# Four recurrent layers: the first head's keys are copied during the projections, the maxima's rows once, and layer 0's V product moves between the first fills

## The reference

```
xn = layernorm(x)
# layer 0
q, k, v = xn @ Wq + bq, xn @ Wk + bk, xn @ Wv + bv      # 16 heads of 8
attn = softmax(q @ k.T / sqrt(8));  s = (attn @ v) @ Wo + bo
g = silu(tanh(xn @ weight @ aux1 @ aux2 + bias))
x = x + s * g
# layers 1 and 2: other attentions and feed-forwards, not touched by the change
# layer 3
q, k, v = rope(xn @ qw), rope(xn @ kw), xn @ vw          # 16 heads of 8
s = (causal_softmax(q @ k.T / sqrt(8)) @ v) @ ow;  g = silu(top1_experts(xn))
x = x + s * g
```

## Time and profile before

| | us |
|---|---|
| median of 3 runs | 2002.25 |
| the three runs | 1996.25, 2002.25, 2002.73 |
| profiled execution, its own time | 1996.94 |
| its span, first to last instruction | 1995.1 |
| PE busy in the span | 1650.5 (83%) |
| DVE busy | 1448.0 (73%) |
| ACT busy | 1112.2 (56%) |

### The profile page before, as it was taken

How to read it: one execution, slowest core, us unless ns; L and a number is a source line. 1 busy time by engine, 2 the same in 40 slices (tenths; PEclk the granted TensorE clock), 3 DMA queues, 4 the chain that set the end, 5 groups by cost and what they waited for, 6 DMA issues and landing times. The chain is left out here.

```text
span 1995.1 us, 29288 instructions
## 1 busy us (share of the span) xinstructions
PE 1650.5 (83%) x10105; PEld 666.2 (33%) x10105; DVE 1448.0 (73%) x2724; ACT 1112.2 (56%) x2262; POOL 313.7 (16%) x464
## 2 busy tenths in 40 slices
PE   3689999999999976799987986881659888999877
PEld 2212222222222214344444444771412222222246
DVE  5689999999999905855556056336768889999825
ACT  3258888888888881322212533342306666777744
POOL 0102100100010000000003345313012222111123
PEclk9779999999999997999987988886759999999989
DMA  4001111211110021063223587531501111111132
GB/s 132 32 20 63 66 51 45 73 61 46 46 61 32 4 47 66 5 127 94 93 105 112 154 285 252 184 114 49 182 33 46 47 41 45 42 45 52 32 78 69
DMA packets 80283, 156.07 MB, mean 78 GB/s; under 512 B 20476, under 2 KB 37756, under 8 KB 76440
## 3 DMA queue, kind: packets, MB, share of 16 engines
q1 hardware_dynamic: 65394, 123.90, 19.3%
q0 software_dynamic: 14384, 29.29, 4.9%
q10 hardware_dynamic: 358, 1.01, 0.2%
HBM read 104.33 MB, written 48.89 MB: 77 GB/s over the span
## 5 line engine op out<-in xcount | busy, mean ns | idle before, releaser
L855 ACT ACTIVATE heads_probs<-heads_pS 128x512 f32<-128x512 f32 (+3 forms) x1664 | 822.5, 578 | 217.9 <-PE heads_pS L768 195.5
L880 DVE TENSOR_REDUCE heads_run_max<-heads_pM 128x1 f32<-128x1024 f32 x512 | 601.0, 1219 | 37.0 <-PE heads_pM L742 29.1
L786 PE MATMUL heads_pO<-heads_probs,heads_vh 128*32 128x512 f32 (+2 forms) x3328 | 446.3, 583 | 2.1 <-ACT heads_probs L855 1.4
L768 PE MATMUL heads_pS<-heads_qs,heads_ks 59*128 59x512 bf16 (+3 forms) x1040 | 310.5, 371 | 30.4 <-ACT heads_probs L855 16.0
L742 PE MATMUL heads_pM<-heads_ks,heads_qs 56*128 56x512 bf16 (+3 forms) x1040 | 281.8, 380 | 17.3 <-DVE heads_run_max L891 7.1
L891 DVE TENSOR_REDUCE heads_run_max<-heads_pM 128x1 f32<-128x512 f32 x384 | 246.6, 684 | 18.9 <-PE heads_pM L742 17.8
L742 PE MATMUL heads_pM<-heads_ks,heads_q_first 56*128 56x512 bf16 x624 | 173.3, 397 | 44.1 <-DMA heads_ks<-k_parts_dram 25.8
L768 PE MATMUL heads_pS<-heads_q_first,heads_ks 59*128 59x512 bf16 x624 | 183.6, 376 | 23.8 <-ACT heads_probs L855 18.9
L768 PEld LDWEIGHTS heads_pS<-heads_qs,heads_ks 59*128 59x128 bf16 x1040 | 77.8, 94 | 321.6 <-ACT heads_probs L855 278.6
L888 DVE CUSTOM_DVE_ANT_0 heads_masked_out<-heads_pM,heads_mask_end 128x128 bf16<-128x128 f32 (+3 forms) x256 | 121.0, 486 | 28.5 <-PE heads_pM L742 26.1
L1616 DVE TENSOR_REDUCE second_row_max<-second_banks 128x1 f32<-128x2048 f32 (+15 forms) x16 | 20.7, 1291 | 156.0 <-PE second_banks L1574 77.5
(11 more groups left out here) (384 smaller groups left out, 2139.5 us busy)
## 6 DMA issues: line engine op xcount, KB each, us to landing
top_weights<-k_comb_dram SPq DMA_DIRECT2D x128, 128.0 KB, 3.0
second_w<-in_L_W_dram SPq DMA_DIRECT2D x12, 1024.0 KB, 10.0
heads_ks<-k_parts_dram SPq DMA_DIRECT2D x124, 96.0 KB
k_hid_slots_dram<-k_zeros SPq DMA_DIRECT2D x8, 1152.0 KB, 4.5
k_h_slots_dram<-second_work SPq DMA_DIRECT2D x48, 192.0 KB
second_work<-k_hid_slots_dram SPq DMA_DIRECT2D x48, 192.0 KB
heads_qs<-k_parts_dram SPq DMA_DIRECT2D x40, 192.0 KB
k_parts_dram<-proj_part SPq DMA_DIRECT2D x12, 512.0 KB, 4.7
```

Of the source, the lines that this page charges most:

```text
L768: mm = pe.matmul(pS[:, slot, 0:c1 - c0], ks[c % ROUND][rows, u * P:(u + 1) * P], qs[c % ROUND][rows, c0:c1], start=True, stop=not diag)
L786: mm = pe.matmul(pO[k * 32:k * 32 + VW, int(second), o:BLK], vh[c][:, t, :], probs[u % 2][:, k * BLK + o:(k + 1) * BLK], start=first_chunk ...
L855: act.activation(probs[u % 2][:, k * BLK + c0 - b * BLK:(k + 1) * BLK], pS[:, slot, 0:c1 - c0], ACT.Exp)\
L880: dve.reduce_max(run_max[:, i, blocks[0][0] // 2:blocks[0][0] // 2 + 1], both.rearrange("p k c -> p (k c)"), AX.X).then_inc(taken, 2)
```

## The change

- The first head's keys go into a buffer `K.first_k` during the projections. As each part of k is split, SP copies its eight rows from the part's own tile, once for each place in the stack and for either half: 6 + 6 + 2 DMAs of 8 rows, each group ahead of that part's store. Their ones are set by POOL in the projections. `load_first_keys` and DVE's ones are gone from the head stage.
- Fills always read rows 64 and up, scores rows 0 and up; `turns` is gone. So the maxima's rows are written to the lower half only (three DMAs per head instead of six), and ones are set there only. Both halves of q and k are still loaded.
- Layer 0's V product leaves the projections and becomes four more steps of `FirstFeedForward` (16 steps instead of 12), each of sixteen 128-column matmuls with the bias through the identity, copied by ACT. Three steps stand ahead of the first fill instead of six. POOL takes V only when all steps are done.
- The masks' swapped copies are made for the lower half only.

```diff
@@ -123,9 +122,8 @@
             dve.tensor_scalar(K.neg_above[:, :], masks[:, 0, :], NEG, None, ALU.mult).then_inc(made, 1)
             dve.tensor_scalar(K.neg_below[:, :], masks[:, 1, :], NEG, None, ALU.mult).then_inc(made, 1)
 
-            for to, at in ((slice(0, HALF), slice(HALF, P)), (slice(HALF, P), slice(0, HALF))):
-                dve.tensor_copy(K.ident_swapped[to, :], K.ident[at, :]).then_inc(made, 1)
-                dve.tensor_scalar(K.neg_below_swapped[to, :], masks[at, 1, :], NEG, None, ALU.mult).then_inc(made, 1)
+            dve.tensor_copy(K.ident_low[:, :], K.ident[HALF:P, :]).then_inc(made, 1)
+            dve.tensor_scalar(K.neg_below_low[:, :], masks[HALF:P, 1, :], NEG, None, ALU.mult).then_inc(made, 1)
 
 
 class Norm:
...
+                        for dst, src in first_keys(K, parts[1][a], a):
+                            sp.dma_start(dst, src).then_inc(K.first_loaded[bool(rope)], 16)
                     sp.dma_start(K.parts[w][:, a, :, :], parts[w][a][:, :]).then_inc(stored[w], 16)
                     if rope and (w, a) == (1, 0):
                         load_first_queries(sp)
             for w in range(2):
                 sp.wait_ge(stored[w], 16 * PARTS)
+
+        @block.gpsimd
+        def _(pool):
+            pool.memset(K.first_k[HALF // 2:HALF, :], 1.0).then_inc(ones_in, 1)
 
         @block.tensor
         def _(pe):
...
@@ -374,7 +382,7 @@
                 project(n)
             if rope:
                 pe.wait_ge(routing.counted, 1)
-            for t in range(NT):
+            for t in range(NT if rope else 0):
                 if t % TPB == 0 and t >= 2 * TPB:
                     pe.wait_ge(vkept, t // TPB - 1)
                 mm = pe.matmul(pv[:, t // TPB % 2, t % TPB * P:(t % TPB + 1) * P], K.xnT[:, t * P:(t + 1) * P],
@@ -462,11 +470,6 @@
                     for i, at in enumerate(ROUTE_AT):
                         if at == n:
                             routing.dve_step(dve, i)
-            if not rope:
-                for c in range(NB):
-                    dve.wait_ge(vproj, c + 1)
-                    dst, src = v_block(c)
-                    dve.tensor_tensor(dst, src, bv.unsqueeze(1).broadcast_to([P, TPB, D]), ALU.add).then_inc(vkept, 1)
 
 
 def query_loads(K, h):
...
@@ -487,6 +490,14 @@
     for half in (0, HALF):
         for row, end, src in query_loads(K, 0):
             yield K.first_q[half + row:half + end, :], src
+
+
+def first_keys(K, kept, part):
+
+    n, at = PRODUCTS[part], sum(PRODUCTS[:part]) * HD
+    for half in (0, HALF):
+        for k in range(n):
+            yield K.first_k[half + at + k * HD:half + at + (k + 1) * HD, :], kept[0:HD, :]
 
 
 def causal_plan(causal):
...
         last_stored = S.sem("last_stored")
...
         SECOND = sorted({(k, b) for _, k, _, b, _, _, second in chunks if second})
...
@@ -596,17 +607,11 @@
                 for row, end, src in key_loads(K, h):
                     yield ks[c % ROUND][half + row:half + end, :], src, stacked[c % ROUND]
 
-        def load_first_keys(queue, turn):
-            half = (0, HALF)[turn]
-            queue.wait_ge(ones_set[0], turn + 1)
-            for row, end, src in key_loads(K, 0):
-                queue.dma_start(ks[0][half + row:half + end, :], src).then_inc(stacked[0], 16)
-
         def split_max(queue, g):
 
             queue.wait_ge(splitting, 4 * g + 1)
             if g > 0:
-                queue.wait_ge(rows_in, 32 * PARTS * g)
+                queue.wait_ge(rows_in, 16 * PARTS * g)
             queue.tensor_copy(max_parts[:, 0, :], neg_max[:, :]).then_inc(splitting, 1)
             queue.wait_ge(splitting, 4 * g + 2)
             queue.tensor_tensor(left[:, :], neg_max[:, :], max_parts[:, 0, :], ALU.subtract).then_inc(splitting, 1)
...
@@ -638,10 +643,9 @@
         @block.sync
         def _(sp):
             def load_max_rows(c):
-                for row in (STK, HALF + STK):
-                    for a in range(PARTS):
-                        sp.dma_start(qs[c % ROUND][row + a:row + a + 1, :].rearrange("o (t c) -> o t c", c=P),
-                                     max_rows[a * NT:(a + 1) * NT, :]).then_inc(rows_in, 16)
+                for a in range(PARTS):
+                    sp.dma_start(qs[c % ROUND][STK + a:STK + a + 1, :].rearrange("o (t c) -> o t c", c=P),
+                                 max_rows[a * NT:(a + 1) * NT, :]).then_inc(rows_in, 16)
 
             def one_head(p, c):
                 if exists(p, c + 2):
...
@@ -657,13 +661,12 @@
                     sp.dma_start(dst, src).then_inc(sem, 16)
 
 
-            load_first_keys(sp, 0)
-            sp.wait_ge(ones_set[1], 2)
+            sp.wait_ge(ones_set[1], 1)
             for dst, src, sem in load_stacks(0, 1):
                 sp.dma_start(dst, src).then_inc(sem, 16)
             sp.wait_ge(exped, 1)
             load_max_rows(0)
-            sp.wait_ge(ones_set[2], 2)
+            sp.wait_ge(ones_set[2], 1)
             every_head(one_head)
             for c in range(ROUND):
                 sp.wait_ge(ot_stored[c], 16 * STORES * len(range(c, LAST, ROUND)))
...
@@ -707,15 +710,16 @@
                     scatter.finish(pool)
 
             for i in range(1, ROUND):
-                for n, row in enumerate((HALF // 2, HALF + HALF // 2)):
-                    pool.memset(ks[i][row:row + HALF // 2, :], 1.0).then_inc(ones_set[i], 1)
-                    pool.wait_ge(ones_set[i], n + 1)
+                pool.memset(ks[i][HALF // 2:HALF, :], 1.0).then_inc(ones_set[i], 1)
+                pool.wait_ge(ones_set[i], 1)
             for i in range(ROUND):
                 pool.memset(vh[i][:, :, HD:VW], 0.0).then_inc(zeroed, 1)
             pool.wait_ge(zeroed, ROUND)
             for i in range(ROUND):
                 pool.memset(vh[i][:, :, HD:HD + 1], 1.0).then_inc(v_preset, 1)
             pool.wait_ge(v_preset, ROUND)
+            if feed:
+                pool.wait_ge(feed.ffn_kept, feed.STEPS)
             take_v(0, 0)
             if not causal:
                 split_max(pool, 0)
...
@@ -733,12 +735,12 @@
                 n = BLOCKS * (ROUND * p + c) + before[j + 1]
                 i, blocks, _ = runs[j]
                 if j == 0:
-                    pe.wait_ge(stacked[c % ROUND], 16 * LOADS * (p + c // ROUND + 1))
+                    loads = LOADS * (p + c // ROUND + 1) + (FIRST_LOADS - LOADS if c % ROUND == 0 else 0)
+                    pe.wait_ge(stacked[c % ROUND], 16 * loads)
                 if not isinstance(n, int) or n > FILLED:
                     pe.wait_ge(taken, n - FILLED)
                 for k, (b, w) in enumerate(blocks):
-                    at = next(turns)
-                    rows = slice(at, at + STK)
+                    rows = slice(HALF, HALF + STK)
                     mm = pe.matmul(pM[:, bank_of(c, j, k), 0:w], qs[c % ROUND][rows, i * P:(i + 1) * P],
                                    ks[c % ROUND][rows, b * BLK:b * BLK + w], start=True, stop=True)
                 mm.then_inc(filled, 1)
...
@@ -759,17 +761,16 @@
                 e = EVENTS * h + place(p, c, n) + 1
                 slot = (EVENTS * c + place(p, c, n) + 1) % RING
                 if n == 0:
-                    pe.wait_ge(rows_in, 32 * PARTS * (h + 1))
+                    pe.wait_ge(rows_in, 16 * PARTS * (h + 1))
                 if not isinstance(e, int) or e >= RING:
                     pe.wait_ge(exped, e - RING + 1)
                 diag = causal and c0 == u * P
-                at = next(turns)
-                rows, mask = slice(at, at + STK + PARTS), slice(at, at + HALF)
+                rows, mask = slice(0, STK + PARTS), slice(0, HALF)
                 mm = pe.matmul(pS[:, slot, 0:c1 - c0], ks[c % ROUND][rows, u * P:(u + 1) * P],
                                qs[c % ROUND][rows, c0:c1], start=True, stop=not diag)
                 if diag:
                     pe.matmul(pS[:, slot, 0:P], K.ident_b[mask, :], K.neg_below[mask, :], start=False, stop=False)
-                    mm = pe.matmul(pS[:, slot, 0:P], K.ident_swapped[mask, :], K.neg_below_swapped[mask, :], start=False,
+                    mm = pe.matmul(pS[:, slot, 0:P], K.ident_low[:, :], K.neg_below_low[:, :], start=False,
                                    stop=True)
                 mm.then_inc(scored, 1)
 
...
@@ -809,7 +810,7 @@
                                 turn(p, c + 1, (EVENTS * (ROUND * p + c) + TURN_AT + 1, (EVENTS * c + TURN_AT + 1) % RING))
                             score_chunk(p, d, n)
 
-            AT_ONCE = 6
+            AT_ONCE = 3
             for m in range(AT_ONCE if feed else 0):
                 feed.pe_step(pe, m)
             pe.wait_ge(preset, 1)
...
@@ -957,11 +955,13 @@
             w, moving = ((K.w["L0_ffn_weight"], K.xnT), (K.w["L0_ffn_aux_weight1"], self.probs[0]))[n]
             mm = pe.matmul(self.ring[:, m % ring, :], w[:, :], moving[:, cols], start=True, stop=True)
         else:
+            still, w, bias = ((self.probs[1], K.w["L0_ffn_aux_weight2"], K.row["L0_ffn_bias"]),
```

(14 more changed lines are left out.)

29 lines of the change are left out of this document (14 added, 15 removed).

## The result

The changed kernel takes **1973.15 us** (median of 4 runs, 1972.4 to 1979.2) beside 2002.49 for the kernel before (4 runs, 1996.25 to 2003.7): ratio **0.9869, interval 0.9847 to 0.9891**, faster by 1.3%. The forecast was 1974. Its profiled execution took 1973.72 (span 1971.9), 23.2 us less than before's.

A forecast was written before the change was run, and what follows sets the result against it. It took a 2.39 us ring through ACT and PE as the bound, plus late maxima rows and slow starts. Terms -16.0 - 0.9 - 7.3 = -24.2 from 1996.94 gave 1972.7; 1.3 on top made 1974 us, range 1964 to 1989.

The forecast's parts named there:

- The rows (-16.0): Heads of layers 0 and 3: three maxima DMAs instead of six remove PE's waits, 9.0 plus 7.0 us.
- The margin of 1.9 us: At each head's change: three row issues take 2.9 us where six needed 4.8, leaving 1.9 us spare.
- Fixed halves at no cost in the unit: Heads' units of fills and scores: fixed halves cost 0, with 0.12 us margin, and the unit stays 2.39 us.
- The rival of pairs on one half: Heads of layers 0 and 3: same-half pairs delay the fourth score, 37 us in all, 2011 us; chance 0.06.
- Layer 0's projections (+3.7): Layer 0's projections: fourteen key copies on SP and crowded DMA engines delay the head stage to 56.0, +3.7 us.
- the first rival: Projections of layers 0 and 3: copies at 1.2 us per issue start both stages 10 us later, 1985 to 1990; chance 0.13.
- Layer 0's start (-9.35 + 4.8): Layer 0's head stage: first fill 9.35 us sooner after stage start, then 4.8 us lost to feed steps and halves.
- the warm slots: Layer 0's first fills: warmer early slots return about 1 us of the loss.
- Layer 3's start (-7.3): Layer 3's start: stage start 4.7 us later, first fill 12.0 sooner within the stage, net -7.3 us.
- the -12.0: Layer 3's head stage: DVE ready at 1453.7, where before the first fill ran at 1465.72, -12.0 us.
- The bound of -4: Layer 3's start: the weaker bound on its net gain, -4 us, if issues take 0.75 us.
- Sum: Whole kernel: rows, layer 0's start and layer 3's start add to -24.2 us, giving 1972.7 for the profiled execution.

The follow-up runs named there:

- e9: The kernel before, unchanged, run again with a trace in the third group: ratio 1.0006 to the kernel before.
- e10: The changed kernel, unchanged, run again with a trace in the third group: ratio 0.9869 to the kernel before.
- e1: The kernel before with fixed halves and three rows of maxima instead of six, nothing else: ratio 0.9957 to the kernel before.
- e2: The changed kernel with the maxima's rows written to both halves again, six DMAs per head: ratio 0.9903 to the kernel before.
- e3: The changed kernel with layer 0's V product back in the projections, twelve feed-forward steps: ratio 0.9880 to the kernel before.
- e4: The changed kernel with fills on the lower half too, where the scores are: ratio 1.569 to the kernel before.
- e5: The changed kernel with the stores of k's three parts ahead of all fourteen key copies on SP: ratio 0.9880 to the kernel before.
- e7: The changed kernel with the first head's queries also copied from part tiles, copies shared among SP, ACT and POOL: ratio 0.9882 to the kernel before.
- e6: The changed kernel with fills on both halves in turn until the first score: ratio 0.9848 to the kernel before.
- e12: The kernel before with fixed halves alone, still six rows of maxima: ratio 1.0054 to the kernel before.

## Why the prediction was right, and where not

**The rows (-16.0): measured -16.3 on the heads from the first transpose on (-8.2 and -8.1).** The size is right for this pair of executions; in e9 and e10 layer 0's fourteen periods give 8.9, as here 8.7, but layer 3's heads 14.3, since the kernel before takes 407.3 us there and not 401.2. Three rows are enough for it: e1's fourteen periods take 541.55 although packets of code still fall 0.7 to 6.9 us behind the first twelve of its transposes and its third row lands up to 3.4 us after its issue. The margin of 1.9 us took them up, as reckoned. The cause was given wrongly. I wrote of "anything that slows one issue", and read the issue of 3.43 us at 1544.78 as SP's own. In fact a load of program code kept one engine of the sixteen; the row whose packets queue behind it lands late, in layer 3 SP's next issue waits as well, and which head is hit depends on where the code's loads fall. And it was not asked what else of the change moves them: with V between the fills nearly all have moved away, so that even six rows don't stall in layer 0 (e2). Either of the two, three rows (e1) or the rest of the change (e2), removes layer 0's 9 us; together they give them once. That the whole gain came out near 16 although its cause was misread is in part luck. In the whole change three rows are therefore needed only for some 3 to 5 us of layer 3 (397.6 in e2 against 393 to 395). That the place of the packets and not the level of that group did it is supported by e1 and e3, of the same group, whose packets fall on the rows as in the kernel before.

**Fixed halves at no cost in the unit: right.** 38.62 per undisturbed head in every trace but e4's. The rival of pairs on one half fell; its price appears where I had not put it, in e4, where the granted clock stays at 0.50 with it.

**Layer 0's projections (+3.7): measured +4.5**, stage start 52.31 to 56.83. The sum was near for wrong terms, which is luck. Issues cost 0.79 us each and not 0.5 (most 0.62 to 0.67, two of them 1.3 and 1.5), so the last store left at 50.59 and not near 46.6. It landed in 5.3 and not in 10.7 us: the first queries' last packets (queue q10) move between 53 and 54 us as in the kernel before, so the later store meets only the end of them, while e5's last store, issued at 38.95, took 10.9 again. That is half of the first rival's mechanism without its size. (That rival's own sum does not come out: 10 us later in both stages is 20 and not 12 to 15, so 1994, outside the range.) The Trainium skill, "DMA: Bandwidth & Descriptors", section "Issuing engines are not separate DMA queues", calls the issue time "usually small relative to the DMA itself". For one DMA the trace agrees, 0.58 us of issue against 5.3 of landing for the last store; but fourteen issues on one queue add up to 11.12 us, and that set the end. By the same section of the Trainium skill, issuing from several engines saves only the issue time. In e7 it gained 5 us in layer 3, and in layer 0 the issues themselves grew longer and it lost 5.

**Layer 0's start (-9.35 + 4.8): measured -10.05 and +4.1.** The first fill comes 4.80 us after the stage starts, and from there to the first transpose it is 44.88 us instead of 40.80. The terms: V was 1.4 and is 2.2 by e3; halves were 3.2 + 1.2 = 4.4 and are 3.6 by e6; 5.8 less 4.1 leaves 1.7 for the warm slots, which no run shows alone. The warm clock was a small term of -1 in my sum. e12 shows that it counts for more: without the early keys the same halves cost 8 us.

**Layer 3's start (-7.3): measured -4.0, in e10 -5.1.** This is the step that failed in size. The first fill gained -11.65 against the stage's start, near the -12.0. But the stage starts 7.6 us later, counted from its projections, and not 4.7. The term that was mis-sized is the time that SP takes to issue the copies: they were priced at 0.5 us, six of them 3.0, and the fourteen took 11.5 us (0.82 each, single ones up to 1.74), the last store 2.22 more. So that store left 11.7 us later than before, counted from the projections, and landed in 5.9 us instead of 10.0. The bound of -4 was laid for "issues of 0.75 us", and that is what came.

**Sum.** -24.2 predicted for the profiled execution, -23.2 measured, of which the touched stretches give -21.8 and the untouched -1.4. The gain is 23.2 us between the two profiled executions, 29.3 between the medians and 26.2 by the ratio, so that the median came within 1 us of the forecast is luck. The touched terms together missed by 2.4 us.

## What to carry to other kernels

When a small DMA lands late now and then, look in the DMA view of that window for a packet of program code before blaming its queue; such loads can move with an edit elsewhere in the program (here with V's place, while e1 and e12 left them where they were), so put the parts of a change back one by one before crediting one with the gain. Running small matmuls in turn on both halves paid most where PE had just waited: at 1.2 GHz fills on one half occupied PE completely (8.00 of 8 us in e12). Price the copies that are added to one queue at the longer issue times of that stage (0.79 us here), and add them up.
